# Adding a tile's products to the output sum one step later in two long attentions

## What is computed

```python
Q = (query @ W_q).reshape(b, m, H, D_K).transpose(0, 2, 1, 3)      # H = 16, D_K = 64, m = 64
K = (key_value @ W_k).reshape(b, n, H, D_K).transpose(0, 2, 1, 3)  # n = 6272
V = (key_value @ W_v).reshape(b, n, H, D_V).transpose(0, 2, 1, 3)
scores = jnp.einsum('bhmk,bhnk->bhmn', Q, K)
attn = jax.nn.softmax(scores / np.sqrt(D_K).astype(np.float32), axis=-1)
ctx = jnp.einsum('bhmn,bhnv->bhmv', attn, V)
```

## Time and profile before

| | us |
|---|---|
| median of 3 runs | 407.27 |
| lowest and highest run | 406.82, 411.14 |
| the profiled execution | 406.98 |
| its span, first to last instruction | 405.1 |
| outside the span | 1.88 |

### The profile page before, as it was taken

The page is one execution under the profiler, slowest core; times in us unless marked ns, Lnnn a source line. Parts: engine busy times, 40 slices in busy tenths (PEclk is TensorE's granted clock), DMA queues, the critical chain, the costliest instruction groups (busy, mean ns, idle before and its releaser), DMA issues.

```text
span 405.1 us, 11383 instructions
## 1 busy us (share of the span) xinstructions
PE 383.4 (95%) x4529; PEld 280.0 (69%) x4529; DVE 276.8 (68%) x715; ACT 287.2 (71%) x568; POOL 256.4 (63%) x207
## 2 busy tenths in 40 slices
PE   6988899999999999989999999998999999999996
PEld 3435677777777778954955767776777768867843
DVE  2796788888887776566767766676776666454544
ACT  3478768888888887646439988999888987534240
POOL 2489988999975659201007989999999879030000
PEclk9899999999999999999999999999999999999999
DMA  8899979999999999990006999999999999700000
GB/s 308 323 256 154 198 142 199 160 184 208 182 190 212 228 201 155 354 391 2 3 2 105 203 190 191 196 186 194 173 194 211 183 195 179 302 2 2 3 1 5
DMA packets 188389, 68.55 MB, mean 169 GB/s; under 512 B 183200, under 2 KB 183984, under 8 KB 187440
## 3 DMA queue, kind: packets, MB, share of 16 engines
q1 hardware_dynamic: 188048, 66.77, 82.1%
q10 hardware_dynamic: 288, 1.05, 0.7%
HBM read 21.90 MB, written 0.03 MB: 54 GB/s over the span
## 4 chain that ended last, share of the span: by engine, by line
PE 47%; POOL 19%; DMA 11%; DVE 9%; ACT 6%; issue 5%; SPq 0%; POOLq 0%; DVEq 0%; ACTq 0%
PE ps L522 16%; POOL halves L594 14%; PE ps L490 13%; DMA probsT<-halves 10%; DVE probs L641 3%; PE ps L1106 2%; PE ps L502 2%; PE ps L768 2%; ACT probs L559 2%; DMA moe<-in_ctxT 2%; ACT halves L566 2%; PE ps L1214 1%; PE ps L828 1%; PE ps L942 1%; PE ps L773 1%
## 5 line engine op out<-in xcount | busy, mean ns | idle before, releaser
L594 POOL TENSOR_TENSOR halves<-probs,halves 128x896 f16<-128x896 f32 x84 | 160.8, 1924 | 36.1 <-ACT halves L566 34.9
L522 PE MATMUL ps<-ctxN,probsT 128*128 128x128 f16 x2352 | 148.6, 219 | 5.9 <-DMA probsT<-halves 5.8
L522 PEld LDWEIGHTS ps<-ctxN,probsT 128*128 128x128 f16 x2352 | 139.0, 98 | 20.7 <-issue 10.4
L490 PE MATMUL ps<-ctxT_parts,GT_parts 128*128 128x512 f16 (+1 forms) x660 | 142.9, 353 | 3.7 <-DVE negmax L641 3.5
L559 ACT ACTIVATE probs<-probs,shifted 128x896 f32<-128x896 f32 x112 | 115.5, 1031 | 7.2 <-DVE shifted L646 7.2
L490 PEld LDWEIGHTS ps<-ctxT_parts,GT_parts 128*128 128x128 f16 x660 | 59.9, 98 | 54.4 <-DVE negmax L641 5.4
L566 ACT CAST halves<-probs 128x896 f16<-128x896 f32 x93 | 85.9, 923 | 0.1
L654 DVE SCALAR_TENSOR_TENSOR U<-U,alpha,ps 128x128 f32<-128x128 f32 x112 | 38.7, 345 | 60.4 <-PE ps L522 60.3
L641 DVE CUSTOM_DVE_ANT_0 probs<-ps,maskb,negmax 128x896 f32<-128x896 f32 x56 | 67.5, 1206 | 3.7 <-POOL halves L594 3.3
L641 DVE CUSTOM_DVE_ANT_0 probs<-ps,zero,negmax 128x896 f32<-128x896 f32 x56 | 67.5, 1206 | 2.1 <-POOL halves L594 1.6
L556 ACT ACTIVATE alpha<-negmax 128x1 f32<-128x1 f32 x96 | 28.3, 295 | 36.8 <-DVE negmax L641 36.3
(11 more groups left out here) (369 smaller groups left out, 381.2 us busy)
## 6 DMA issues: line engine op xcount, KB each, us to landing
moe<-in_ctxT SPq DMA_DIRECT2D x7, 448.0 KB, 7.5
moe<-in_mask SPq DMA_DIRECT2D x6, 448.0 KB, 9.9
moe<-in_gateT SPq DMA_DIRECT2D x2, 1024.0 KB, 9.2
moe<-in_upT SPq DMA_DIRECT2D x2, 1024.0 KB, 11.0
moe<-in_downT SPq DMA_DIRECT2D x2, 1024.0 KB, 12.6
moe<-in_fir_long SPq DMA_DIRECT2D x1, 2048.0 KB, 10.5
probsT<-halves SPq DMA_TRANSPOSE x93, 4.8
wv<-in_wv SPq DMA_DIRECT2D x2, 512.0 KB, 6.8
```

The lines of the kernel that those rows point to most:

```text
L490: ins = pe.matmul(ps[:, 2 * b + h, 0:width], GT_parts[:, g_part, r * P:(r + 1) * P], ctxT_parts[:, keys:keys + width], start=(g_part == 0 ...
L522: ins = pe.matmul(ps[:, bank, 0:D], probsT_parts[:, b, p_part, k * P:(k + 1) * P], ctxN_parts[:, at:at + D], start=(p_part == 0 and c_part ...
L594: eng.tensor_tensor(halves_of(L, n)[:, 1, :], probs[:, n % BUFS, :], halves_of(L, n)[:, 0, :], ALU.subtract).then_inc(lower_of(L, n)[0], 1)
```

## The change

One number is changed. `ADD_LAG` goes from 6 to 7 for both attentions, so VectorE issues add(i-7) in iteration i, behind maximum(i), where it issued add(i-6) before.

```diff
-PV_LAG, ADD_LAG = 5, 6
+PV_LAG, ADD_LAG = 5, 7
```

## The result

| | before | after |
|---|---|---|
| median of 20 runs, us | 406.98 | 409.36 |
| lowest and highest run | 405.82, 411.14 | 408.82, 410.36 |
| the profiled execution | 406.98 | 409.85 |
| its span | 405.1 | 408.0 |

The ratio after to before is 1.0061, with a 95% interval from 1.0048 to 1.0075. The kernel became 2.4 us slower, which is within 1%. It was forecast to become 2.5 us faster.

What follows compares the result with a forecast made beforehand. The prediction took TensorE, busy for 95% of the span, as the bound. Its terms -4.9, -1.4 and +3.8 sum to -2.5 us against 406.98, giving 404.5 us; the range was 400.7 to 410.2.

Steps and rivals of the forecast that it cites:

- First term: Second attention: the maximum starts up to 1.47 us earlier, so TensorE's waits for the turning DMA mostly go; -4.9 us.
- the whole chain behind it follows as long as no stage is full: Second attention: exponentials, GpSimd's lower half and the turning DMA move earlier with the maximum, by up to 1.47 us.
- Second term: First attention from 60 us: TensorE's wait for a maximum and one for a DMA go, with refills; -1.4 us.
- Third term: End of each attention: pv(51) and pv(53) wait for adds behind lower halves; 1.7 and 2.1 us, together +3.8.
- T: End of the second attention: when TensorE starts turning tiles 53 and 54, 341.99 us in the profile before.
- The 0.1 us for the signal and the first weights: End of the second attention: estimated delay from the end of add(49), T + 2.67, to pv(51), near T + 2.80.
- the third rival: First attention: VectorE's and GpSimd's lower halves collide, eight times 0.76 us, 6.1 in all; 410.6 us, chance 0.06.
- the second: Ends of both attentions cost nothing, because lower halves of 53 and 55 come a microsecond earlier; 400.7 us, chance 0.12.
- The first rival: Second attention: landings don't move, lateness being GpSimd's or the DMA's own; the ends' price stays; 410.2 us, chance 0.20.

Runs made afterwards that it cites:

- Half the DMA: Against the kernel before, the DMA turns only upper halves in the second attention and the matmuls use them twice; 403.0 us, ratio 0.9896.
- the later adds: Adds seven steps late until the last scores, then as before; 405.61 us against the kernel before, 399.73 us together with half the turning DMA.
- half of GpSimd's product: Against the kernel before, GpSimd makes the lower half of only the first 448 columns in the second attention; 406.18 us, ratio 0.9987.

## Why the prediction was wrong

**First term, the second attention: forecast -4.9, measured +0.7 within a scatter of about 1.** The step that failed is "the whole chain behind it follows as long as no stage is full". A stage was full, and it was not GpSimd, the one that the prediction looked at: it was the turning DMA, seen in SyncE's issues. Its share of 1.07 stood in the earlier trace rows and was not read; but the first attention, where the DMA isn't the bound, has the same 1.07, so the share by itself would not have told. A tile of both halves is 128 x 2 x 896 values of 2 bytes, 458,752 bytes. At the 206 GB/s of a stretch without a load of instructions it takes 2.23 us, at the 189 with one 2.43; the issues follow each other every 2.43 us, and TensorE wants a tile every 2.31. So the DMA falls behind by about a tenth of a us per tile, and TensorE makes up for it in its waits. Without the loads it would just about keep up, an estimate from these rates that no run tried. SyncE's own part of an issue is not the bound, since an issue can take 1.3 us. A maximum that comes 1.43 us earlier (2.77 - 1.34) let a tile wait 1.3 us longer in front of SyncE. The term was sized from the longest single wait against the gain of the maximum, as if the waits were chance delays of a chain; they were the lack of one stage's rate, and such a lack is the same however early the tiles come. Half the DMA shows it from the other side: 4.55 us of the second attention go without a change of order, and 5.59 with the later adds (132.07 - 126.48), which is the size that the prediction gave to the waits, 5.2.

The Trainium skill, in "DMA: Bandwidth & Descriptors", section Latency and other measured facts, gives 261 GB/s for a transposing DMA whose middle dimension isn't contiguous, the lower of its two figures; by it a tile would take 1.76 us, an estimate, and the DMA would not be the bound. The trace's 206 and 189 GB/s decide here.

**Second term, the first attention: forecast -1.4, measured -1.47.** The two waits at the earlier trace rows went, as argued. There one tile in four is turned on TensorE, so the DMA has room (31 issues from 59.6 to 159.5 us, one every 3.3), and what was late was VectorE. With the order of before kept at the end, the stretch gives 1.89. That the forecast fits to 0.1 us is in part luck: with the order of before the turning of 53 and 54 starts anywhere from 160.90 to 162.30 us in five traces (161.00 in the one that the prediction read), with later adds from 159.48 to 159.92 in five.

**Third term, the ends: forecast +3.8, measured 1.63 + 2.00 = 3.63 in the two traces, and by itself 3.88 in the trace and 3.1 to 5.4 by the runs.** The steps came one by one: pv(51) at T + 2.73 for T + 2.80, pv(53) at 349.51 - 342.87 = T + 6.64 for T + 6.75. The 0.1 us for the signal and the first weights stands in no row; after the change add(49) ends at 345.21 + 0.34 = 345.55 and pv(51) starts 0.05 us later. The wait of 1.03 us for an add that stood behind a lower half is what the rule of order in "Perfetto Trace Analysis" (the Trainium skill) makes of it (section Tensor Engine Instruction (MATMUL, LD_WEIGHTS)), so the trace agrees. No wait stands between 62 and 160 us, so the third rival, colliding lower halves, did not come; the second, ends that cost nothing, is ruled out by these waits.

**The rivals.** The first rival, that the landings don't move, is what happened; it gave 410.2 us, against the profiled 409.85 and the median 409.36. Its condition was right ("the lateness of a turned tile is GpSimd's or the DMA's own"), but its chance was weighed by GpSimd alone, and half of GpSimd's product shows that GpSimd had no part. It also took only 0.6 us of gain for the first attention, where the whole 1.4 came, because there the DMA was not full.

**What stays open.** Why an unchanged second attention takes 131.1 us in one execution and 132.1 in another, and where the 1.0 us goes that the later adds seem to cost it, the runs don't tell.

## What to carry to other kernels

Before a wait for a DMA is put down to the chain that feeds it, look at the queue that issues it. Issues that begin when the one ahead ends, that take longer than the shortest of them, and whose pace stays when their tiles are ready earlier, were the sign here that the transfer itself was the full stage. Compare the rate of that stage with the step of the engine that waits; if it is slower, only less to transfer or another route helps, and the other route costs what it costs. A lag in a software pipeline can have one length in the steady part and another at the end: here one number for both gave a loss of 2.4 us, and the same lag with the end as it was, in one attention, a gain of 2.5.

## What the hardware showed

- The issue of a transposing DMA on SyncE took from 1.3 us to 4.3, and 1.53 with no other in flight; with half the bytes nearly every one took 1.22.
- Tiles of 458,752 bytes were issued every 2.42 or 2.43 us, whether they stood ready in front of SyncE for 0.8 us, 2.0 or 2.1.
- A load of 16 KB of TensorE's instructions goes with a gap of some 1.5 us in the turning DMA, longer than the 0.95 us of the load itself; with 33 score and product instructions in a step in place of 27 the loads came every 9.4 us in place of every 11.
- In a stretch whose DMA was full, neither 43 us less work for GpSimd (120.19 to 76.96) nor a maximum 1.43 us earlier gained anything on TensorE that could be measured.
